# A four-layer graph network on one core: shares and an added row kept in PSUM in the stages that finish one layer and begin the next

## The reference

```python
h = relu(layernorm(x)); x = x + gat(gat_relu(h))        # layer 0: two attentions, 4 heads, own-edge term
h = relu(layernorm(x)); x = x + dot_attention(h)        # layer 1: 8 heads, q, k, v
h = relu(layernorm(x)); x = x + edge_messages(h)        # layer 2
h = relu(layernorm(x)); x = x + weighted_attention(h)   # layer 3
# gat_conv: h = x@W; e = leaky_relu(a_s[src] + a_d[dst]); ex = exp(e - max over dst)
#   out = segment_sum(h[src] * ex / segment_sum(ex)) + b        (b: the row added to x, b2 of the second one)
# layer 2: msgs = silu(concat(h[src], edge) @ W + b)
#   out = layernorm(segment_sum(msgs)) * gamma + beta           (beta: the row added to x)
```

## Time and profile before

| | |
|---|---|
| median of 3 runs | 7287.14 us (7276.08 to 7295.61) |
| profiled execution | 7288.54 us, span 7286.7 us |
| mean granted TensorE clock | 0.804 of full speed |
| busy: PE, DVE, ACT, POOL | 4903.0, 5215.1, 3534.8, 4987.7 us |
| HBM traffic | 128 GB/s over the span |

### The profile page before, as it was taken

The page is one execution under the profiler, slowest core; times in us unless marked ns, Lnnn a source line. Parts: engine busy times, 40 slices in busy tenths (PEclk is TensorE's granted clock), DMA queues, the critical chain, the costliest instruction groups (busy, mean ns, idle before and its releaser), DMA issues. The chain is left out here.

```text
span 7286.7 us, 123600 instructions
## 1 busy us (share of the span) xinstructions
PE 4903.0 (67%) x21121; PEld 3548.6 (49%) x21122; DVE 5215.1 (72%) x11952; ACT 3534.8 (49%) x8063; POOL 4987.7 (68%) x4990
## 2 busy tenths in 40 slices
PE   5463257777627777776777777768898972677775
PEld 4452145555415555554555555546666651444443
DVE  7665267777737777787888888866666564777777
ACT  4342157777627777743444444423333321666664
POOL 0475677777577777757877778667777761777773
PEclk9855578888868888888988889878888875777777
DMA  5422244444425444435666666534444432544443
GB/s 173 50 69 44 70 129 135 135 135 136 95 56 136 136 135 135 135 79 155 183 178 179 182 180 180 149 94 121 120 120 121 119 81 62 137 136 136 135 136 87
DMA packets 625330, 906.00 MB, mean 124 GB/s; under 512 B 345945, under 2 KB 399862, under 8 KB 624794
## 3 DMA queue, kind: packets, MB, share of 16 engines
q0 software_dynamic: 248160, 655.67, 33.0%
q1 hardware_dynamic: 376666, 223.78, 12.1%
q10 hardware_dynamic: 416, 25.60, 1.1%
HBM read 869.74 MB, written 61.59 MB: 128 GB/s over the span
## 5 line engine op out<-in xcount | busy, mean ns | idle before, releaser
L2303 POOL DMA_INDIRECT ae_ring<-tab_a,ae_idx x816 | 839.3, 1029 | 279.5 <-issue 260.1
L1444 POOL DMA_INDIRECT at_ring<-tab_s,at_idx x816 | 775.6, 951 | 309.1 <-issue 204.8
L1444 POOL DMA_INDIRECT at_ring_0a<-tab_s,at_idx_0a x816 | 779.7, 956 | 273.4 <-issue 203.3
L1444 POOL DMA_INDIRECT at_ring_0b<-tab_s,at_idx_0b x816 | 778.5, 954 | 273.2 <-issue 204.4
L1924 POOL DMA_INDIRECT ad_ring<-tab_qv,ad_idx x816 | 780.8, 957 | 265.4 <-issue 213.4
L1603 PE MATMUL at_po<-at_rows,at_hot 128*128 128x260 f32 x1632 | 558.7, 501 | 110.2 <-DVE at_begin L103 85.0
L2124 PE MATMUL ad_pk<-node_a,ad_hr 128*128 x1632 | 471.0, 439 | 219.1 <-DVE ad_prod L1996 121.4
L1603 PE MATMUL at_po_0a<-at_rows_0a,at_hot_0a 128*128 128x264 f32 x1632 | 512.4, 467 | 113.2 <-DVE at_begin_0a L103 91.6
L1603 PE MATMUL at_po_0b<-at_rows_0b,at_hot_0b 128*128 128x264 f32 x1632 | 512.3, 467 | 113.0 <-DVE at_begin_0b L103 93.7
L2422 PE MATMUL ae_pM<-ae_we,ae_featT 64*128 64x256 f32 x1632 | 476.2, 439 | 118.4 <-DVE ae_pre L2385 118.4
L575 POOL DMA_INDIRECT recs_s<-rnk_recs_now,rnk_pos_now x294 | 287.1, 977 | 359.0 <-DVE rnk_both L478 269.7
(11 more groups left out here) (501 smaller groups left out, 12490.8 us busy)
## 6 DMA issues: line engine op xcount, KB each, us to landing
at_rr_0a<-relrow_d SPq DMA_DIRECT2D x102, 256.0 KB
at_rr_0b<-relrow_d SPq DMA_DIRECT2D x102, 256.0 KB
ad_rr<-relrow_d SPq DMA_DIRECT2D x102, 256.0 KB
ae_feat<-attr_pad SPq DMA_DIRECT2D x816, 32.0 KB
at_rr<-relrow_s SPq DMA_DIRECT2D x102, 256.0 KB
rnk_lrow<-lorow_f SPq DMA_DIRECT2D x98, 256.0 KB
attr_pad<-in_edge_attr_dram ACTq DMA_DIRECT2D x1, 25000.0 KB, 79.4
at_ring_0a<-tab_s,at_idx_0a POOLq DMA_INDIRECT x816
```

The source lines that it names most:

```text
L1444: eng.indirect_dma_start(out=ring[:, t.slot * STEP + u, :], out_offset=None, in_=table, in_offset=bass.IndirectOffsetOnAxis(ap=idx[:, t.sl ...
L2303: eng.indirect_dma_start(out=ring[:, k, :], out_offset=None, in_=table, in_offset=bass.IndirectOffsetOnAxis(ap=idx[:, k:k + 1], axis=0))\
```

## The change

In every renew with one matrix (M == 1) two PSUM banks more are allocated. The shares and the own shares are kept in the first, the row that ahead adds in the second. The product of line 908 is written there directly; the shares are copied there by one instruction; the row, loaded by DMA to SBUF as before, is copied to PSUM once at i == -2. Share, self_share and ahead then take their second operand from PSUM. With three matrices the SBUF tiles are used as before. The wait for the weights at i == -2 is made in one place for all kinds.

```diff
-            beta = sb(f"rn_beta_{tag}", [P, D], F32, c)
+            beta_in = sb(f"rn_beta_{tag}", [P, D], F32, c)
...
+            if M == 1:
+                shared = ps(f"rn_shares_{tag}", [P, 2, 512], c)
+                part = shared[:, 0, 0:NB * 8].rearrange("p (b h) -> p b h", h=8)
+                self_part = shared[:, 0, NB * 8:NB * 12].rearrange("p (b h) -> p b h", h=4)
+                beta = shared[:, 1, 0:D]
+            else:
+                part, self_part, beta = s, r, beta_in
...
                         if gat:
-                            st.own(eng, eng.tensor_tensor(r[:, :, :], r[:, :, :], s[:, :, 0:4], ALU.mult))
+                            st.own(eng, eng.tensor_tensor(self_part[:, :, :], r[:, :, :], s[:, :, 0:4], ALU.mult))
+                        if M == 1:
+                            st.own(eng, copy(eng, part[:, :, 0:H], s[:, :, 0:H]))
...
-                        did("share", b, eng.tensor_tensor(agg(b), agg(b), spread(s[:, b, 0:H], H, F), ALU.mult))
+                        did("share", b, eng.tensor_tensor(agg(b), agg(b), spread(part[:, b, 0:H], H, F), ALU.mult))
...
-                        did("self", b, eng.tensor_tensor(node, node, spread(r[:, b, :], H, F), ALU.mult))
+                        did("self", b, eng.tensor_tensor(node, node, spread(self_part[:, b, :], H, F), ALU.mult))
...
-                        did("ahead", b, eng.tensor_tensor(x_sb[:, b, :], x_sb[:, b, :], beta[:, :], ALU.add))
+                        did("ahead", b, eng.tensor_tensor(x_sb[:, b, :], x_sb[:, b, :], beta, ALU.add))
...
                     def score_weights():
-                        eng.wait_ge(wl, 16 * n_w)
...
                         if i == -2:
+                            eng.wait_ge(wl, 16 * n_w)
                             if scores:
                                 score_weights()
-                            elif b_aps or vecs:
-                                eng.wait_ge(wl, 16 * n_w)
+                            if addend is not None and M == 1:
+                                st.own(eng, copy(eng, beta, beta_in[:, :]))
...
                     if addend is not None:
-                        eng.dma_start(beta[:, :], addend.to_broadcast([P, D])).then_inc(wl, 16)
+                        eng.dma_start(beta_in[:, :], addend.to_broadcast([P, D])).then_inc(wl, 16)
```

## The result

The changed kernel takes 7205.87 us (median of 4 runs, 7195.63 to 7206.72), the kernel before beside it 7281.61 us (4 runs, 7274.12 to 7295.61): a ratio of 0.9891, 95% interval 0.9872 to 0.9909. That is 76 us where 37.5 were forecast. The profiled execution of the changed kernel took 7206.20 us, its span is 7204.2 us, its mean granted clock 0.81.

A forecast was written before the change was run, and what follows sets the result against it. Renew 0b was taken as bound by POOL, its scatter held 39.89 us by DVE's two-SBUF-input run. 37.1 + 0.4 = 37.5 us off 7288.5 gave 7251.0 us, range 7236 to 7271.

The forecast's parts named there:

- Step 1: Renew 0b: PSUM operands for shares, own shares and added row free POOL's held scatters, gaining 37.1 us (33.4 to 38.9).
- rival B: Renew 0b: POOL wins the port and DVE waits, so only 18 us are gained: 7271 us; chance 0.05.
- Step 2: Renews 0b and 2: a PSUM operand costs DVE zero; the skill's page would give 3.2 us in renew 2.
- Steps 3 to 5: Renews 0b and 2: copies add 0.75 us each, covered in 0b; renew 2 nets 0.4 us gain; moved weights wait, zero.
- Step 6: Four later loops: shifted place in memory costs zero, within 0.3 us each, 1.2 us either way over all.
- the rivals: POOL stays held, 7289 us (0.10); DVE waits for POOL, 7271 us (0.05); repeated PSUM columns read slowly, 7316 us (0.03).

The follow-up runs named there:

- e8_free_mid: Kernel before plus one single-input DVE reduction inside renew 0b's two-SBUF-input run, edge loop padded to 2944: within 0.3% of the kernel before's 10012.18 us on a slow chip.
- e3_2_only: Changed kernel with the PSUM change in renew 2 alone, no-ops keeping the edge loop at 2944: 7217.41 us, ratio 0.9936 to the kernel before.
- e1_place: Kernel before with four empty DVE instructions behind renew 2 and four fewer behind renew 3: 7247.72 us, ratio 0.9956 to the kernel before.
- e2_0b_only: Changed kernel with the PSUM change in renew 0b alone, edge loop at 2942: 7242.72 us, ratio 0.9945 to the kernel before.
- e4_row_only: Changed kernel with the change in renew 0b alone and only the added row read from PSUM, shares left in SBUF: 7242.89 us (one run).
- g1_swap: Changed kernel with the first sum of each last-edge-aggregation turn issued before its first one-hot: 7173.38 us, ratio 0.9865 to the kernel before.
- f3_nops: Kernel before with three empty DVE instructions ahead of renew 0b's two-SBUF-input run, edge loop at 2944: 7208.69 us, ratio 0.9912 to the kernel before.

## Why the prediction was wrong, by its own steps

**Step 1, POOL's stall: right, in cause and size.** 37.1 us were forecast and 36.8 came; the wait at the barrier fell from 72.4 to 35.3 us, 35 forecast; the last scatter ended within 0.3 us of where it was worked out, counted from the stage's start. e8_free_mid shows the mechanism directly. What I didn't see is that the stall is there only in some executions. One profile can't show that, and the three times beside it all seem to be of the upper kind too. Against executions that aren't held (renew 0b 90.4 us in e3_2_only, 89.7 in the changed kernel), this step gains next to nothing; that the kernel before was held where it was measured beside the changed one is luck for the number. The Trainium skill, page "SBUF — State Buffer", section "SBUF: two separate sides", says of the pair of ports that whoever starts first has it for one whole instruction. For a DVE instruction with two SBUF inputs it says so only against a GpSimd instruction that reads SBUF, a condition that my prediction left out, and it infers that such an instruction doesn't keep GpSimd from writing descriptors; the 39.89 us and e8_free_mid say otherwise. POOL held over 115 starts of DVE instructions in a row goes beyond the rule of one instruction as well, and scatters that pass between the same instructions without slowing them (417 to 419 ns in e3_2_only) don't look like it at all; rival B, which I had built on that sentence, didn't happen.

**Step 2, PSUM operands: right in effect.** Nothing on the path. The 0.02 us that each of the 125 instructions of renew 0b got longer fall on those without PSUM as well, and other executions with the same edit don't have them. (The starts 0.33 us apart "behind either" in the earlier trace rows are behind lines 933 and 986; line 915 isn't in those rows.) In renew 2 lines 924 and 985 take 403 and 400 ns, where 915 and 976 took 408 and 407. The 65 ns that I had estimated from the page "VectorE: DVE Perf Modes" of the Trainium skill aren't seen on any of these lines.

**Steps 3 to 5: right within their bounds.** Renew 2 takes 79.9 us in place of 79.2, a loss of 0.7 us where I took a gain of 0.4 between 1.6 gained and 0.75 lost: near the end of the loss. The scatters didn't get quicker (1001 ns each, 990 before). Whether the copies cost the 0.7 us isn't shown: renew 2 takes 80.4 to 80.6 us in e1_place, e2_0b_only and e4_row_only, where its operands are as before, and 79.5 in g1_swap, where they are changed. One line of DVE did get slower, the scale:

```profile
L615 POOL DMA_INDIRECT recs_s<-sc_recs_rn,sc_pos_rn x54 | 54.1, 1001 | 35.1 <-DMA sc_pos_rn<-edge_pos 19.0 <-issue 16.2
...
L966 DVE TENSOR_SCALAR rn_hn<-x_sb,rn_mv,rn_rstd 128x256 f32<-128x256 f32 x25 | 11.8, 472 | 0.0
```

It took 407 ns before and in f3_nops and 473 in e3_2_only, but also 463 in e1_place and e2_0b_only, where renew 2 reads no share from PSUM. So it isn't the change that does it; what does wasn't tried.

**Step 6, the loops behind: this is the step that failed.** It set four loops to zero, within 0.3 us each, by the two attends of the earlier trace rows. They agree in time although DVE's gaps in them don't (70.8 us in all in attend 0b, 68.9 in 0a): the granted clock of both is 0.82, and the 1.9 us didn't move it. Why an attend doesn't amplify wasn't tried. I took the one pair of loops that could be compared for the price of place everywhere, and carried it over to two loops with other turns, whose own rows I hadn't looked at. They were in the trace of before: a gap of "issue" at the head of all 51 turns, turns of two lengths, 39 of 49 of them the long one, and PE's clock falling once a turn. From these I could have seen that a change of that gap may count many times over (six- to nine-fold in the runs: 34.2 us for 6.0, 35.9 for 4.1). The size of the shift of place couldn't have been forecast from the trace, nor its sign; but the bound for this loop should have been the 39 long turns at some 1.5 us, 58 us of gain, and the ten short ones, 15 us of loss, and not 0.3. The range was too narrow by that. attend_dot's 8.0 us belong to the same zero, with their cause open.

**The sum.** With 36.9, 8.0 and 2.5 us for the loops in place of zero, 7288.5 - 36.8 + 0.7 - 47.4 = 7205.0, and the rest of the stages, with rounding, gives the 1.2 us to 7206.2. That the two halves are nearly equal is chance. None of the rivals occurred; the right rival, "what is moved in memory is worth as much as what is saved", was missing.

## What to carry to other kernels

An edit that adds instructions moves every loop behind it, so look at each of those loops for a gap at the head of its turn and for turns of two lengths before you set its price to zero; and test it by empty instructions alone, as in e1_place, before you credit the edit. Where TensorE idles once a turn and its clock falls there, a tenth of a microsecond in each turn may be worth six to nine times itself, and shortening the head of the turn can pay more than its own time (34 us for 16 in g1_swap). On DVE, an unbroken run of instructions with two SBUF inputs may shut POOL's DMAs out for the whole run; one operand in PSUM in every few instructions ends it (none held in renew 0b with three in five, 1.37 us at most with one in five), and as it doesn't happen in every execution, the times of several runs belong beside the profile.

## What was new about the hardware

- A DMA of POOL beside a run of DVE instructions with two SBUF inputs is either held for the whole run (39.89, 39.91 us) or passes at 1.04 us each, in the same code. A held one ends 0.91 to 1.03 us behind the start of the first other instruction (16.66 and 23.27 us long in e8_free_mid).
- Where a loop lies in DVE's program changes the gap at the head of its turn and can open one inside it: 1.30 us at 2940 and 2941, 1.22 at 2942, 2944, 2960 and 3004, and at 2942 another 0.22 us ahead of the last two adds.
- 0.1 us in a turn of 20.6 moved the granted clock of a loop between 0.86 and 0.89 and 34 to 37 us of its time: faster by its place, slower again by empty instructions. 0.3 us taken out by another order moved the clock from 0.89 to 0.90 and 34 us.
- On one chip the same kernel took 10012 us in place of 7261 to 7287, at a clock of 0.69 to 0.74; the four kernels run beside it there (two with the change, two without) are all within 0.3% of it.
